# Attention and mixture-of-experts block on one core: order of VectorE's side work, five shared units first, last sums on GpSimd

## The reference

```
x = x + layernorm(linear_attention(layernorm(x)))      # 16 heads, elu feature maps, gated running state
x = x + layernorm(moe(layernorm(x)))

moe(x):
    gate_out = x @ gate_w                               # 8 experts
    top_v, top_i = top_k(gate_out, 2)                   # softmax over the two gives their weights
    out = sum over the two experts of swiglu(x, ew1[e], ew2[e], ew3[e]) * weight
    out = out + swiglu(x, sw1, sw2, sw3)                # the shared expert, for every row
swiglu(x, w1, w2, w3):
    h = x @ w1                                          # 256 -> 512
    return h * sigmoid(h) * (x @ w2) @ w3               # 512 -> 256
```

## Time and profile before

| | |
|---|---|
| timed runs | 806.1, 795.51, 793.99 us; median 795.51 |
| profiled execution | 802.89 us, its span 801.1 us |
| granted TensorE clock, mean | 0.977 of full |
| busy in the span | TensorE 722.1, weight loads 604.8, VectorE 557.3, ScalarE 462.7, GpSimd 483.4 us |
| chain that ended last | TensorE 35%, VectorE 12%, issue 6%, ScalarE 4%, GpSimd 2% |

### The profile page before, as it was taken

How to read it: one execution, slowest core, us unless ns; L and a number is a source line. 1 busy time by engine, 2 the same in 40 slices (tenths; PEclk the granted TensorE clock), 3 DMA queues, 4 the chain that set the end, 5 groups by cost and what they waited for, 6 DMA issues and landing times.

```text
span 801.1 us, 25500 instructions
## 1 busy us (share of the span) xinstructions
PE 722.1 (90%) x8863; PEld 604.8 (75%) x8863; DVE 557.3 (70%) x1129; ACT 462.7 (58%) x1030; POOL 483.4 (60%) x705
## 2 busy tenths in 40 slices
PE   5779989898999988786999999999999999999982
PEld 4567767776877766575888889999999986688871
DVE  4898888998899899678766644434444434358996
ACT  3556766565666555733455576566666657544552
POOL 4133334877588767664860188887666666626764
PEclk9999989999999999999999999999999999999996
DMA  8335332444344434887431222112232222327986
GB/s 260 94 78 134 107 98 82 127 137 128 94 142 128 122 94 147 283 251 192 140 118 35 45 55 55 41 42 68 81 94 75 78 77 80 108 86 200 205 168 107
DMA packets 58251, 93.27 MB, mean 116 GB/s; under 512 B 7216, under 2 KB 36784, under 8 KB 58128
## 3 DMA queue, kind: packets, MB, share of 16 engines
q1 hardware_dynamic: 41664, 61.72, 27.4%
q0 software_dynamic: 10288, 21.51, 10.0%
q10 hardware_dynamic: 6176, 8.40, 3.6%
HBM read 59.60 MB, written 32.01 MB: 114 GB/s over the span
## 4 chain that ended last, share of the span: by engine, by line
PE 35%; DVE 12%; issue 6%; ACT 4%; POOL 2%; DVEq 1%; ACTq 0%; POOLq 0%; another core or an unknown queue 0%
PE bank L1324 20%; PE bank L1368 11%; PE bank L1344 3%; DVE bank L1720 2%; DVE wpart L1624 2%; DVE wtmp_p L1674 2%; PE bank L1308 1%; ACT gh L1423 1%; DVE stc L1687 1%; DVE gl L1711 1%; DVE xl L1728 1%; POOL rsc L1853 1%; ACT chosen L1460 1%; DVE wtmp_p L1670 1%; POOL xs_scratch L573 1%
## 5 line engine op out<-in xcount | busy, mean ns | idle before, releaser
L1324 PE MATMUL bank<-xh,W 128*128 128x256 f16 x1504 | 260.5, 274 | 19.4 <-DVE gl L1711 12.6
L1324 PE MATMUL bank<-xl,W 128*128 128x256 f16 x752 | 206.3, 274 | 0.0
L1324 PEld LDWEIGHTS bank<-xh,W 128*128 (+1 forms) x1504 | 148.2, 99 | 43.5 <-issue 14.9
L1423 ACT ACTIVATE gh<-bank 128x512 f16<-128x512 f32 x103 | 61.2, 595 | 150.4 <-DVE bank L1720 137.3
L1368 PE MATMUL bank<-W,gh 128*128 (+1 forms) x824 | 139.4, 274 | 4.1 <-DVE wtmp_p L1670 4.1
L1711 DVE TENSOR_TENSOR gl<-bank,gh 128x512 f16<-128x512 f32 x103 | 70.9, 689 | 68.5 <-ACT gh L1423 63.8
L1826 POOL DMA_INDIRECT yt_scratch<-ysh,dest x71 | 75.9, 1069 | 69.0 <-POOL dest L1820 44.9
L1368 PE MATMUL bank<-W,gl 128*128 (+1 forms) x412 | 113.0, 274 | 0.0
L573 POOL DMA_INDIRECT xs_scratch<-xn_all,posi x64 | 88.5, 1382 | 27.5 <-issue 15.1
L1720 DVE SCALAR_TENSOR_TENSOR bank<-sl,w_scale,bank 128x512 f32<-128x512 f32 x94 | 70.9, 754 | 48.0 <-PE bank L1324 34.1
L619 PE MATMUL bank<-xnT,wT 128*128 128x256 f32 x384 | 92.4, 391 | 1.6 <-ACT xnT L371 1.6
(11 more groups left out here) (204 smaller groups left out, 1392.8 us busy)
## 6 DMA issues: line engine op xcount, KB each, us to landing
W<-gate_scratch SPq DMA_DIRECT2D x64, 256.0 KB
ysh<-yt_scratch SPq DMA_DIRECT2D x16, 512.0 KB, 4.9
xt<-xs_scratch SPq DMA_DIRECT2D x31, 260.0 KB
W<-in_L_ffn_ew_dram ACTq DMA_DIRECT2D x15, 512.0 KB, 3.9
W<-in_L_ffn_ew_dram SPq DMA_DIRECT2D x9, 512.0 KB, 8.5
x_in<-in_L_attn_x_dram SPq DMA_DIRECT2D x16, 256.0 KB, 4.3
out_dram<-x SPq DMA_DIRECT2D x16, 256.0 KB
xT_scratch<-xn2T SPq DMA_DIRECT2D x16, 256.0 KB
```

What stands on the lines that cost most here:

```text
L1324: last = mm(dst[n % 2][:, i * R:(i + 1) * R], W16[:, e, m, s, at:at + P], a[:, k, :], start=(k == 0 and s == 0 and a is x_h), stop=(k == K ...
L1423: act.activation(gh[t.u % 2][h][:, :], (pH1 if t.kind == "single" else pH2)[n % 2][:, :], ACT.Copy)\
```

## The change

The first silu moves ahead of a `yield`, so that it is issued at the end of the attention stage's pass C+1 and not in the next. `EARLY` is 5: five shared units stand ahead of the routed ones and eleven behind them, T0 is 45, and six steps are kept. `beside` does the tables first, in eight calls rather than five, then the largest values one a gap in all three gaps; the scales of experts 2 and 3 come in gap 2 of turn 6 (in turn 3 before), those of experts 4 to 8 as before in gap 1 of turn 12. The last single is projected and taken out in pass T0 itself. The sum with the shared expert's row of kept steps goes from VectorE to GpSimd, which counts both sums in `mix1`.

```diff
--- before.py
+++ after.py
@@ -46,7 +46,7 @@
     RING, LANES = 28, 4
-    EARLY = 6
+    EARLY = 5
     assert (B, GR, KC, TOPK) == (2, 2, 2, 2) and C % 2 == 0 and HC * D == MW
@@ -1176,7 +1176,7 @@
             return [t for t, lag in ((unit_at(u - 2), 2), (unit_at(u - 1), 1))
-                    if t is not None and lag == (2 if t.kind == "single" else 1)]
+                    if t is not None and lag == (2 if t.kind == "single" and t.u < T0 - 1 else 1)]
@@ -1195,6 +1195,13 @@
+        def sums_upto(c):
+
+            return sum(1 if from_bank(k) else 2 for k in range(c + 1))
+
+        def bank_sums_upto(c):
+            return sum(from_bank(k) for k in range(c + 1))
+
         def entry(eng, row, t, least, most):
@@ -1219,7 +1226,7 @@
-        SHARE = (2, 11)
+        SHARE = (5, 11)
@@ -1248,7 +1255,7 @@
                         need_rows(sp, j)
-                need(sp, U["mix1"], c - 1)
+                need(sp, U["mix1"], sums_upto(c - 2))
                 sp.dma_start(ya[c % 2].rearrange("p b k d -> p b (k d)"), yt_by_step[order[c]]).then_inc(ya_loaded[c % 2], 16)
@@ -1357,7 +1364,7 @@
                 elif t.u >= 2:
-                    pe.wait_ge(U["mix2"], order.index(units[t.u - 2].n) + 1)
+                    pe.wait_ge(U["mix2"], bank_sums_upto(order.index(units[t.u - 2].n)))
                 for h in range(t.halves):
@@ -1392,10 +1399,15 @@
                     turn_x(following)
-                late = [y for y in projected(u) if y.kind == "single" and t is not None and t.kind == "shared"]
-                for y in late:
+                late = projected(u) if u == T0 else []
+                for y in late[:-1]:
                     project(y, e_of.pop(y.u))
-                if t is not None:
+                if u == T0:
+                    turn_gated(prev)
+                    hidden(t, e_of[u], 0)
+                    project(prev, e_of.pop(prev.u))
+                    hidden(t, e_of[u], 1)
+                elif t is not None:
                     if t.kind == "single":
@@ -1506,8 +1518,8 @@
             load_matrices()
+            silu(one, 0, e_of[0])
             yield
-            silu(one, 0, e_of[0])
             act.wait_ge(w_low, 5)
@@ -1529,9 +1541,14 @@
                 for y in projected(u - 1):
-                    e = e_of.pop(y.u)
-                    if y.routed or y.n <= EARLY:
-                        rows_out(y, e)
+                    if u - 1 != T0:
+                        e = e_of.pop(y.u)
+                        if y.routed or y.n <= EARLY:
+                            rows_out(y, e)
+                if u == T0:
+                    high_g(prev, 0)
+                    for y in projected(u)[:-1]:
+                        rows_out(y, e_of.pop(y.u))
                 if following is not None:
@@ -1540,12 +1557,14 @@
                     silu(t, 0, e_of[u])
-                if prev is not None and prev.kind == "single":
+                if prev is not None and prev.kind == "single" and u != T0:
                     high_g(prev, 0)
                     high_g(t, 0)
+                    if u == T0:
+                        rows_out(prev, e_of.pop(prev.u))
                     silu(t, 1, e_of[u])
@@ -1576,6 +1595,8 @@
                 link(V.tensor_copy(pairs, te_i[:, :]))
+
+            def pairs_of_experts():
                 link(V.tensor_tensor_scan(cum, pairs, zero, 0.0, A_, A_))
@@ -1599,12 +1620,16 @@
                 link(V.tensor_tensor(work, slot, by_slot(te[0:1, 6:8, :]), ALU.is_ge))
+
+            def one_owner_of_slots():
                 link(V.tensor_tensor(tg[:, 0], tg[:, 0], tg[:, 1], ALU.subtract))
                 link(V.tensor_reduce(tb[:, 1, :], tg[:, 1], AX_X, ALU.add))
+
+            def numbers_of_slots():
                 link(V.tensor_tensor(tg[:, 2], tg[:, 0], iota8[0:1, :].unsqueeze(1).broadcast_to([1, 2 * SLOTS, E]),
@@ -1634,44 +1659,37 @@
+            tables = [tiles_of_experts, pairs_of_experts, rows_of_experts, owners_of_slots, one_owner_of_slots,
+                      experts_of_slots, numbers_of_slots, rows_of_slots]
+
             def beside(u, gap):
-                turn, n = 3 * (u - 1) + gap - 1, 2 * (u - 4) + gap // 2
-                if turn < 3:
-                    largest_of(*pieces[2 * turn])
-                    largest_of(*pieces[2 * turn + 1])
-                    if turn == 2:
+                turn = 3 * (u - 1) + gap - 1
+                n = turn - len(tables)
+                if turn < len(tables):
+                    tables[turn]()
+                elif n < first_group:
+                    largest_of(*pieces[n])
+                    if n == first_group - 1:
+                        assert u == SHARE[0]
                         largest_of_group(1)
-                elif turn == 3:
-                    tiles_of_experts()
-                elif turn == 4:
-                    rows_of_experts()
-                elif turn == 5:
-                    owners_of_slots()
-                elif turn == 6:
-                    experts_of_slots()
-                elif turn == 7:
-                    rows_of_slots()
+                elif n == first_group + 2:
                     scales(link, dve, spread_b[0], 1)
                     scales(link, dve, spread_b[1], 2)
-                elif gap != 1 and n < len(rest):
-                    largest_of(*rest[n])
-                    if n == len(rest) - 1:
+                elif n - first_group - (n > first_group + 2) < len(rest):
+                    k = n - first_group - (n > first_group + 2)
+                    largest_of(*rest[k])
+                    if k == len(rest) - 1:
                         assert u == SHARE[1]
             def add_rows(c):
-                a = cmb[:, c % MIXED].rearrange("p b d -> p (b d)")
-                dve.wait_ge(U["mix1"], c + 1)
-                t = shared[order[c]]
+                dve.wait_ge(U["mix1"], sums_upto(c))
                 if from_bank(c):
+                    a, t = cmb[:, c % MIXED].rearrange("p b d -> p (b d)"), shared[order[c]]
                     dve.wait_ge(T["y_done"], t.u + 1)
                     V.scalar_tensor_tensor(a, pYB[t.u % 2][:, :], w_scale[:, 2, 0:1], a, ALU.mult, ALU.add)\
-                     .then_inc(U["mix2"], 1)
-                else:
-                    dve.wait_ge(T["yo_ready"], rows_upto(t.u))
-                    V.tensor_tensor(a, a, ysh[:, B * t.n:B * (t.n + 1), :].rearrange("p b d -> p (b d)"), ALU.add)\
                      .then_inc(U["mix2"], 1)
@@ -1683,7 +1701,8 @@
                 for b in range(B):
-                    dve.wait_ge(U["mix2"], c + 1)
+                    if from_bank(c):
+                        dve.wait_ge(U["mix2"], bank_sums_upto(c))
                     V.bn_stats(stc[c % 2][:, b, :], cmb[:, c % MIXED, b, :]).then_inc(U["stat1"], 1)
@@ -1846,6 +1865,12 @@
                     .then_inc(U["mix1"], 1)
+                if not from_bank(c):
+                    t = shared[order[c]]
+                    pool.wait_ge(U["mix1"], sums_upto(c) - 1)
+                    pool.wait_ge(T["yo_ready"], rows_upto(t.u))
+                    pool.tensor_tensor(cmb[:, c % MIXED], cmb[:, c % MIXED], ysh[:, B * t.n:B * (t.n + 1), :], ALU.add)\
+                        .then_inc(U["mix1"], 1)
```

## The result

The changed kernel takes 815.44 us (median of 4 runs, 811.96 to 819.13); the kernel before, run beside it, 797.16. The ratio is 1.0189, interval 1.0133 to 1.0244; a second comparison gives 1.0196 (1.0134 to 1.0258). The forecast was 803.4, a ratio of 1.010. The direction is right, the size half of what came. The interval reaches over 2%, so the runs leave open whether this is "within" or "slower" by the prediction's own limit. Ratios are of the faster runs of each kernel, and the profiled executions of four variants (the silu alone, the last single, gaps 1 and 2, tables first with six units) are among their slower ones, so that a length from those weighs less.

A forecast was written before the change was run, and what follows sets the result against it. Bounds: TensorE without idle time from 464 to 655 us, VectorE's rounds between pairs and in the tail. Terms: +8.0 at the tail's start, -3.9, +2.8, +1.0, so +7.9: 803.4; forecast range 798 to 810, term bounds 789 to 815.

The forecast's parts named there:

- "within" or "slower": Outcome classes, with about 2% (16 us) as the limit: within had chance 0.80, slower 0.16.
- Split of the second expert: GpSimd's later split of expert 2's weights holds up the fifth pair's load, TensorE standing: 8.6 us lost.
- Rival (a): The split is no wait, the tail starts 0.6 sooner and gains 3.9: 791.0; chance 0.28 together with (d).
- (b): Reductions cost the rounds nothing and all idle time of 345 to 464 us goes: 778.6; chance 0.04.
- (d): The parts do nothing that can be measured: 795; chance 0.28 together with Rival (a).
- Three reductions a round: VectorE's rounds between pairs take 10.1 us with three reductions, bounds 8.9 to 10.1.
- First silu sooner: At the attention stage's end, silu and table load fit a ScalarE wait; routing and all after come 1.4 us sooner.
- Tables first: First pair's load out at 377.6, transposes 9.0 us sooner, one shared unit less behind it: net about 1 us.
- TensorE's slower restart +1.0: TensorE restarts slower after its long stop: +1.0 us (0 to 2).
- Tail: With GpSimd's sums double rounds fall from 9.61 to 8.4 us; tail 100.1 against 104.0, so -3.9.
- late scatters: GpSimd's last scatters end later, so rows are summed at 734.4 where the first mixing round wants 731.6: +2.8 us.
- Rival (c): GpSimd bounds the tail, its sums blocking VectorE; over 2% slower, 820.8; chance 0.18, whole or in part.

The follow-up runs named there:

- the packed run: The changed kernel with the six reductions of experts 2 and 3 packed two a gap into turn 4, exchange in pass 4: ratio 1.0052.

## Why the prediction was right in direction and half the size

All times are against H, which takes 3.42 off the changed kernel's.

- **Split of the second expert: right, in mechanism and nearly in size.** A wait of TensorE ends 3 us behind the split. It is 7.05 long and not over 10, since the stop one pair ahead took a part: it is 14.40 where that one is down to 1.48. D(8) - D(4) is 49.6 for 47.7 forecast. The parts alone lack this wait and sum to +2.5; together they give 12.9. Rival (a) falls, and (b) with it, for TensorE stands more and not less; the interval of the ratio leaves (d) out.
- **Three reductions a round: right**, 10.17 and 10.09 to 10.1. The prices by gap fit too: gaps 0 and 2 give 8.9, and the third reduction, in gap 1, adds 1.25. Gaps 1 and 2 give 8.3, which is also TensorE's pace.
- **First silu sooner: the step that failed.** "-1.4" became +1.8: D(1) is 22.1 behind H, 20.25 before. The table came at 332.6 against H as forecast, and the statistics 1.4 sooner. But in this trace, and in all but one of those with the silu moved, TensorE's clock fell behind its stop for 9 to 11 us. The half of the hidden layer behind the gate products took 5.12 for 2.78, and the prefix products, queued behind that half, came 2.5 later. At D(4) the move costs 2.6 (53.9, and 51.3 with the silu back).
- **Tables first: mechanism right, the number by luck.** SP's load had waited for the scatters before, and does so again. D(4) is 53.9 behind H, forecast 52.2, 1.6 late. The silu accounts for 4.0 (-1.4 became +2.6), so something else was 2.3 too long. Most of it is the 1.5 that I put between the last scatter's landing and the load. Before, that scatter was issued at 373.02 and landed at 377.5 by my reading, 4.5 later; in the changed kernel the load goes out 4.1 behind the last scatter's issue (382.73 - 378.64), so there is no 1.5.
- **Left out: SP's exchange.** I followed the scales and never asked what SP does for them in pass 5. It costs in two ways. It holds the fourth pair back by 8.48, which the split hides behind its own stop; with six units first it is the whole stop of 7.40. And it lands too late for the scales: VectorE waits 1.86 for it (1.50 in the second execution). That is the 1.9 by which D(8) - D(4) is over the forecast of 47.7: with no wait of the scales it is 47.77, with 0.18 (exchange in pass 6) 47.95, with 1.50 it is 49.39.
- **"TensorE's slower restart +1.0": somewhat small, and counted for one stop.** The prediction has two, of 8 to 9 and of over 10 us; there are three, of 5.0, 8.5 and 7.1. Behind them the projection takes 4.95 for 2.78, the hidden layers 6.96 and 6.72 for 5.40, the transposes 1.1 for 0.6 each: 2.2 + 1.6 + 1.3 + 1.5 = 6.6 us of longer work. Most of it ends in the next stop or lies beside VectorE's rounds. On the path I find 0.5 of transposes ahead of D(4), 0.5 ahead of D(8), and the first round behind the split's stop, 10.81 where the packed run, with no stop there, has 10.09: 1.7 in all, inside the 0 to 2 that I gave.
- **Tail: right, slightly short.** Double rounds 8.65 for 8.4; late scatters +3.3 for +2.8; length of the tail 103.8 for 102.9. Rival (c) falls: GpSimd's sums are the best part of the change. The Trainium skill (SBUF — State Buffer, "SBUF: two separate sides") calls the port pair an exclusive lock. The row of `vec` agrees: it takes 1.15 where a free one takes 0.17, and ends at 757.63, with GpSimd's sum (756.34 + 1.27). That and 0.5 for a `shift` is lost in each double round, which is all the same 1.0 shorter than before.

In sum: the tail's start is 380.0 behind H, forecast 374.9 (705.1 - 330.18), 5.1 late: 1.6 at D(4), 1.9 to D(8), 1.2 to unit 14, 0.4 behind it. The tail adds 0.9, and 1.0 was in the forecast apart: 5.0, so 12.9 and not 7.9. The ratio is 1.9% and not 1.0%. On the 795.51 that the forecast started from that is 810.5, inside the range (789 to 815); 815.44, beside a kernel before of 797.16, lies just outside. The range itself is not the sum of its bounds: with all of them at their ends it would be 784 to 812.

## What to carry to other kernels

Before moving a step earlier or later, list everything it feeds in every queue, and find the consumer with the nearest deadline: the same order cost 5 us alone with six units first and 14 in the changed kernel with five, where the split met its pair a unit sooner. Side work goes into the gaps that other work covers: moving one reduction a round from gap 0 to gap 1 gave 3 us. An exchange between engines on a shared queue has a price of its own, for the loads behind it and for whoever waits for it. And a stop of TensorE counts with the slower work behind it, as far as that lies on the path.

## What the runs showed of the hardware

With the first silu moved, TensorE's granted clock mostly falls around the routing. Stretches of TensorE (length, busy, clock, DMA share, GB/s), first of the changed kernel, then of the run with SP's exchange in pass 6, which has the same instructions there; both begin 10, 14 and 18 us behind H:

```profile
343.60:345.60 2.00, 2.00 (x11) 0.50 0.99 305
347.60:349.60 2.00, 2.00 (x11) 0.50 0.96 254
351.60:353.60 2.00, 2.00 (x12) 0.53 0.55 119
```

```profile
338.98:340.98 2.00, 1.20 (x9) 1.00 1.04 360
342.98:344.98 2.00, 2.00 (x21) 1.00 1.05 270
346.98:348.98 2.00, 1.83 (x18) 1.00 0.65 150
```

0.50 is 1.2 of 2.4 GHz; the stop ahead is 2.35 long in both. In five of the six executions with the silu moved the clock stood at 0.50 for 9 to 11 us, and H to D(4) took 53.8 to 53.9 in the three that can be compared. In the sixth it stayed at 1.00 and H to D(4) took 49.9, 1.4 less than the 51.3 of the run with the silu back: the gain that I forecast. In the eight executions without the move, with a stop of 2.6 to 2.9, the clock stayed up in three and was low for 3 to 7 us in five; it was up again for the half behind the gate products, which took 2.78 in all eight. Why the moved silu meets the long low stretch so often stays open.
